# Rows of the second normalisation on ScalarE instead of VectorE

## The reference

```python
h = _layernorm(x, axis=-1) * (1 + ca) + sa
x = x + ga * attention(h)                 # 16 heads of 16 features
h = _layernorm(x, axis=-1) * (1 + cb) + sb
x = x + gb * ffn(h)                       # 2 shared experts, 16 routed, top 4 of them per token

def _layernorm(x, axis=-1, eps=1e-05):
    m = jnp.mean(x, axis=axis, keepdims=True)
    v = jnp.var(x, axis=axis, keepdims=True)
    return (x - m) / jnp.sqrt(v + eps)
```

## Time and profile before

| | |
|---|---|
| median of 3 runs | 909.97 us (909.76 to 910.23) |
| the profiled execution, its time | 910.85 us |
| its span on the core | 909.0 us |
| PE busy | 846.5 us, 93% |
| DVE busy | 645.1 us, 71% |
| ACT busy | 665.0 us, 73% |
| POOL busy | 396.6 us, 44% |
| TensorE's granted clock, mean | 0.984 of full speed |

### The profile page before, as it was taken

One profiled execution on the slowest core, in us unless ns is written; L12 is line 12 of the kernel. 1 busy time (PEld: TensorE's weight loads), 2 busy tenths in 40 slices (PEclk: granted clock), 3 DMA queues, 4 the chain that ended last, 5 costly groups with the idle time before them and its releaser, 6 DMA issues.

```text
span 909.0 us, 19413 instructions
## 1 busy us (share of the span) xinstructions
PE 846.5 (93%) x7652; PEld 450.6 (50%) x7652; DVE 645.1 (71%) x1252; ACT 665.0 (73%) x1125; POOL 396.6 (44%) x331
## 2 busy tenths in 40 slices
PE   4878887999999999999999999999999999998998
PEld 4322133365445555565545555566555554555455
DVE  7856577677688878777788777876787778544332
ACT  3488777878788788878788787788886777854342
POOL 5373224234544453444635453444535253347353
PEclk9988889999999999999999999999999999999999
DMA  7043500531217102450217102450233300420140
GB/s 252 2 115 104 140 1 30 175 66 48 76 54 206 52 1 89 129 145 26 83 53 206 48 19 82 147 141 13 70 113 105 111 2 3 151 94 1 64 154 25
DMA packets 47290, 77.18 MB, mean 85 GB/s; under 512 B 6392, under 2 KB 41432, under 8 KB 43104
## 3 DMA queue, kind: packets, MB, share of 16 engines
q1 hardware_dynamic: 47200, 75.94, 27.3%
HBM read 63.47 MB, written 12.34 MB: 83 GB/s over the span
## 4 chain that ended last, share of the span: by engine, by line
PE 65%; DVE 18%; ACT 9%; issue 4%; POOL 4%; ACTq 0%; DVEq 0%; POOLq 0%
PE scalar_bank L945 18%; PE down_bank L1106 17%; DVE neg_max L902 7%; PE vector_bank L1025 6%; PE vector_bank L1008 6%; PE scalar_bank L1008 6%; PE vector_bank L945 5%; DVE rows L758 3%; ACT q_aug L692 3%; DVE gelu L889 2%; PE scalar_bank L1037 2%; POOL act_lo L650 2%; PE vector_bank L1043 2%; ACT gelu L741 2%; DVE o_raw L893 1%
## 5 line engine op out<-in xcount | busy, mean ns | idle before, releaser
L902 DVE TENSOR_REDUCE neg_max<-vector_bank 128x1 f16<-128x512 f32 x484 | 305.8, 684 | 51.3 <-PE vector_bank L1008 44.6
L706 ACT ACTIVATE probs<-scalar_bank 128x512 f32<-128x512 f32 x486 | 260.5, 603 | 48.8 <-PE scalar_bank L1008 44.5
L650 POOL TENSOR_TENSOR act_lo<-gelu,act_hi 128x512 f16<-128x512 f32 x144 | 180.7, 1275 | 136.4 <-ACT act_hi L683 123.1
L1106 PE MATMUL down_bank<-down_hi,act_hi 64*128 64x256 f16 x1120 | 179.1, 270 | 1.9 <-DVE rows L877 1.5
L1106 PE MATMUL down_bank<-down_hi,act_lo 64*128 64x256 f16 x1120 | 178.2, 269 | 0.0
L1106 PE MATMUL down_bank<-down_lo,act_hi 64*128 64x256 f16 x1120 | 178.2, 269 | 0.0
L889 DVE TENSOR_TENSOR gelu<-gelu,gates 128x512 f32<-128x512 f32 x128 | 116.7, 928 | 65.8 <-ACT gelu L741 65.2
L1008 PE MATMUL vector_bank<-k_aug,q_aug 64*128 64x512 f16 x484 | 133.6, 392 | 11.1 <-DVE neg_max L902 6.0
L1008 PE MATMUL scalar_bank<-q_aug,k_aug 64*128 64x512 f16 x486 | 134.2, 387 | 5.2 <-ACT f_ring L669 2.4
L741 ACT ACTIVATE gelu<-scalar_bank 128x512 f32<-128x512 f32 x144 | 84.7, 596 | 70.5 <-PE scalar_bank L945 39.4
L1025 PE MATMUL vector_bank<-probs,v_aug 128*32 128x512 f32 x992 | 118.5, 601 | 0.0
(11 more groups left out here) (193 smaller groups left out, 1259.6 us busy)
## 6 DMA issues: line engine op xcount, KB each, us to landing
gates<-gates_by_expert SPq DMA_DIRECT2D x32, 1024.0 KB, 4.9
q_aug<-q_parts SPq DMA_DIRECT2D x90, 64.0 KB, 3.4
k_aug<-k_parts SPq DMA_DIRECT2D x90, 64.0 KB, 4.1
x_pre<-in_x SPq DMA_DIRECT2D x8, 512.0 KB, 5.9
x_post<-in_x SPq DMA_DIRECT2D x8, 512.0 KB, 5.4
out<-x_post SPq DMA_DIRECT2D x16, 256.0 KB, 2.5
gates<-in_w_up SPq DMA_DIRECT2D x4, 576.0 KB, 10.6
gates<-in_w_down SPq DMA_DIRECT2D x4, 576.0 KB, 3.9
```

The lines of the kernel that those rows point to most:

```text
L650: pool.tensor_tensor(act[1][:, c, :], gelu[:, n % NGELU, :], act[0][:, c, :], ALU.subtract).then_inc(s_elo, 1)
L706: scalar.activation(probs[:, n % U, :], src[:], ACT.Exp, scale=SCALE).then_inc(taken[kind], 1)
L902: dve.tensor_reduce(neg_max[:, (u // 2) % TT, at:at + 1], src[:], AX.X, ALU.max, negate=True).then_inc(done, 1)
L1106: ins = pe.matmul(o, act[a][at:at + 64, act_slot(b, c), tok:tok + P], wd[w][at:at + 64, c, :], start=n == 0 and k == 0, stop=c == NEX - 1 ...
```

## The change

The four row instructions of `rows2` leave DVE's queue and become four activations `Identity(scale * x + bias)` in ACT's queue at the same place of the list, with scale = rstd and bias = -mean * rstd for each token. POOL computes the bias, by two more instructions on 128x4 numbers: -mean goes into the place of the variance, ahead of the power, and is multiplied by `rstd` behind it. The first normalisation is as before. The counts of `s_ln2` stay at 12 a batch; `s_rs2` counts 4 instead of 2.

```diff
                 elif kind == "stats2":
-                    power(b, mv[1], rstd[1], s_ln2, s_rs2)
+                    wait(pool, s_ln2, 12, b, 8)
+                    mean, var = mv[1][:, :, 0], mv[1][:, :, 1]
+                    pool.tensor_scalar(rstd[1][:], var, EPS, None, ALU.add).then_inc(s_rs2, 1)
+                    wait(pool, s_rs2, 4, b, 1)
+                    pool.tensor_scalar(var, mean, -1.0, None, ALU.mult).then_inc(s_rs2, 1)
+                    pool.tensor_tensor(rstd[1][:], rstd[1][:], minus_half[:], ALU.pow).then_inc(s_rs2, 1)
+                    wait(pool, s_rs2, 4, b, 3)
+                    pool.tensor_tensor(var, var, rstd[1][:], ALU.mult).then_inc(s_rs2, 1)
...
+                elif kind == "rows2":
+                    wait(scalar, s_rs2, 4, b, 4)
+                    for t in range(TT):
+                        scalar.activation(rows[:, t, :], x_post2[b % 2][:, t, :], ACT.Identity, bias=mv[1][:, t, 1:2],
+                                          scale=rstd[1][:, t:t + 1]).then_inc(s_ln2, 1)
...
-                elif kind == "rows2":
-                    ln_rows(rows, x_post, mv[1], rstd[1], s_ln2, s_rs2, b)
```

## The result

| | before | changed |
|---|---|---|
| median of 4 runs | 910.1 us | 930.9 us (928.62 to 933.46) |
| ratio | | 1.0227, 95% interval 1.0212 to 1.0242 |
| profiled execution: time, span | 910.85, 909.0 us | 933.46, 931.6 us |
| DVE busy | 645.1 us | 617.4 us |
| ACT busy | 665.0 us | 680.1 us |

The change costs 20.8 us on the medians; 16.5 had been forecast. PE has as many instructions as before (7652) and is busy 9.4 us longer, which the forecast had not expected.

A forecast was written before the change was run, and what follows sets the result against it. PE's chain of waits was taken as the bound, with ACT's delay passed on to it. Shifts of 6.3 (batches 2 to 4), 5.8 (5 and 6), 0.8, 2.5 and 1.1 us sum to 16.5: 926.5 us, range 916 to 932.

The forecast's parts named there:

- What bounds the kernel: PE's chain of waits: in batch 3, 4.5 us of rows on DVE cost PE only about 0.6 us.
- rival A: ACT has room and DVE's rows were the bound: PE gains 5.0 us, 905 us; chance 7%.
- The activations: Four row activations on ACT: 580 ns each from measured widths, together 2.0 us a batch.
- When ACT may start: ACT's wait for GpSimd before the rows: 0.1 us in batch 3, 1.2 in 5 and 6; power at 1.04 us.
- The stall is passed on whole: Batches 2 to 4: first `probs` and PE's product behind them come 2.1 us late; nothing comes back, 6.3 us.
- the sum: Shifts of PE and ACT over batches 0 to 7, added up to 16.5 us.
- Behind each place PE is the chain again with all others fed by it, so a shift stays: After each batch's rows: the delay is kept, neither caught up nor enlarged.
- PE's busy time unchanged: Sign of being right: PE waits 2.6 us instead of 0.51 for `probs` in batch 3, but works no longer.
- Batch 7: Rows on ACT delay an `act_hi`, its `act_lo` and the second `gelu`; `z_hi` 1.1 us later.
- Batch 0 and 1: First: ACT waits, then rows and six exponentials before `z_hi`, 2.5 us; second: 2.1 us less PE's vanished DVE waits, 0.8.
- rival C: POOL later in batches 1 to 6: power 1.59 us, last product 0.67; 5.8 us more, 932 us; chance 12%.

The follow-up runs named there:

- e9_no_rows: The kernel before without any row instructions in the second normalisation, PE's transposes waiting for GpSimd's power instead: 907.12 us, ratio 0.9967.
- e1_fill: The changed kernel with 10 to 15 unread products filling PE's wait for ACT in batches 0 to 6: 927.1 us, ratio 1.0185.
- e5_no_pool_wait: The changed kernel with the activations' scale and bias taken from constants, waiting only for the statistics, not GpSimd: 924.68 us, ratio 1.0142.
- e7_halves: The changed kernel with every row instruction cut into two of 128 columns, eight a batch: 941.94 us, ratio 1.0337.
- e6_dve_short: The kernel before with rows of 2 columns instead of 256 on DVE: 908.39 us, ratio 0.997.

## Why the prediction was right in direction and low in size

- **What bounds the kernel.** Right. 3% of the chain on the rows had meant 27 us at most; their worth, read from PE's waits as some 5 us (rival A), was 3.7 (e9_no_rows).
- **The activations.** 580 ns and 2.0 us for four were worked out; 591 ns and 2.07 us measured. The interpolation between 64 and 512 columns held; the Trainium skill's 585 ns (ScalarE: Activation LUTs, section "What ACT_TABLE_LOAD costs") is closer still.
- **When ACT may start.** 0.1 us of wait in batch 3 was forecast, none was there; 1.2 in batches 5 and 6 was forecast, 0.93 and 1.08 were there. The power took 1.03 us in batches 3, 4 and 6, beside maxima that read PSUM; in batches 1, 2 and 5, where it began beside DVE's product, it took 1.43 to 1.44. Neither 1.04 nor 1.59 everywhere was right: the instruction added ahead of it took 0.78 us in the first three and 0.23 in the others, and that decides how much of the power meets the product. The two levels agree with the Trainium skill's exclusive lock of the port pair (SBUF — State Buffer, section "SBUF: two separate sides").
- **The stall is passed on whole.** Right, and shown three ways: with PE's wait filled the shift is 2.1, 2.1, 2.1, 2.7 and 2.9 us; with 1.1 us more on ACT it grows by about that; with the rows behind two of the exponentials most of it goes.
- **The step that failed: the sum priced PE's wait at its own length.** "Behind each place PE is the chain again with all others fed by it, so a shift stays" had no term for what the wait does to PE afterwards. In batches 2 to 6 the clock fell behind it, 1.0 to 1.5 us a batch and 6.6 us in all (the changed kernel's distances less those of e1_fill: 1.47, 0.98, 1.44, 1.47, 1.25). That is the profiled execution, the slowest of four; on the medians the filling was worth 4 to 5. "PE's busy time unchanged" stood among the signs of being right, and it rose by 9.4 us. The rows before the change gave no warning: in the window of 440 to 448 the clock was 1.00, with waits of at most 0.5 us.
- **Batch 7.** 1.1 us forecast, 0.0 measured. The second `gelu` does not wait for the `act_lo` behind the rows but for one before it, which is done in time; the wait of 1.21 us in the earlier trace rows had ended with that earlier one. I had taken the wrong instance of the same line. (The terms as written also come to 835.0, not 835.1.)
- **Batch 0 and 1.** 2.5 and 0.8 forecast, 2.3 and 0.4 measured. In batch 0 ACT waited 1.51 us for GpSimd before the rows, as worked out. The clock was lower there too, at 157 to 162 us, but PE waits for ACT anyway: the shift was 2.3 us at `z_hi` and 2.3 still at the table load of 180 us.
- **What was luck.** The miss on the medians, 4.3 us, looks smaller than the term left out, since batch 7's 1.1 us and some 1 us of small excesses elsewhere stood against it. And 930.9 lies inside the range only because rival C reaches to 932; C's cause, a GpSimd later by 1 us a batch, did not come: its last product took 0.20 us and not 0.67.
- **What remains.** 1.55 us lie ahead of the first changed instruction, with a stretch of lower clock at 35 to 39 us that the profile of before does not have. e5_no_pool_wait has it as well, the other experiments do not, though all do the same up to there; so it is not the change's, and its cause is open. Why the clock falls behind one wait and not behind another of the same length is open too. The changed kernel's four runs spread over 4.8 us with mean clocks from 0.973 to 0.978, the four of before over 1.1 us; 21 more runs of before spread over 3.4.

## What to carry to other kernels

In a pipeline where PE writes banks that another engine frees, an added instruction costs what it does to the next bank due, not what the engine's busy share says: the same 2.06 us, eight times, cost 21 us in one place of ACT's queue and 4 in another, two exponentials further on. A share of the chain is not a gain: take the instruction out, or read the wait behind it, before paying for its move. And where a change gives PE a new wait (here 2.5 us), a slower PE behind it may have to be priced too (here 1.0 to 1.5 us a batch).

## What the hardware did that was not expected

- Waits of PE of 2.5 us (batches 2 to 4 of the change), 3.1 us (batch 0) and 3.7 to 3.8 us (batches 5 and 6) were followed by a few microseconds at 1.2 GHz, but not each time: 2.47 us in batch 1, 2.69 us in e5_no_pool_wait and 3.57 us in batch 2 of e7_halves were not. In these runs the length of the wait does not tell whether the clock falls. In batches 2 to 6 the same wait costs 1.0 to 1.6 us more with the fall than without. The filled wait had none in batches 1 to 6.
- A DVE instruction from SBUF to SBUF of 2 columns takes nearly as long as one of 256 when GpSimd works beside it without a break: 1.20 and 1.24 us at the median, where the shortest took 0.28 and 0.40. In batch 3 of e6_dve_short four take 4.24 us on DVE:

```profile
439.67 4.24 DVE L842 TENSOR_SCALAR rows<-x_post,mean_var,rstd 128x2 f32<-128x2 f32 x4
```

GpSimd meanwhile has instructions of 1.1 us without a break:

```profile
439.37 1.17 POOL L603 TENSOR_TENSOR qk_lo<-f_ring,qk_hi 128x512 f16<-128x512 f32 x1
440.50 3.38 POOL L650 TENSOR_TENSOR act_lo<-gelu,act_hi 128x512 f16<-128x512 f32 x3
```

Each row instruction ends just behind one of GpSimd's: the first at 440.57 and 440.54 us, the second at 441.68 and 441.65. One gets through for each of GpSimd's, about 1.1 us a turn, four turns; the wait, not the width, sets the time. That agrees with the exclusive lock that the Trainium skill describes in the section cited above. In the earlier trace rows the 4.51 us fit the same reading: GpSimd's instructions of 1.16 and 3 x 1.18 us end at 445.38, the rows at 445.53.
